# The values of cross attention: a second load from memory, or a copy on POOL

## The reference, cut to what matters

```python
q, k, v = _make_heads(_layernorm(x), H), _make_heads(ctx, H), _make_heads(ctx, H)
u = jnp.einsum('hbqd,hbkd->hbqk', q, k) * scale / np.sqrt(d_k)
logits = jnp.where(mask, -jnp.inf, jnp.tanh(u) * jnp.exp(log_C))
attn = jax.nn.softmax(logits, axis=-1)
out = jnp.einsum('hbqk,hbkd->hbqd', attn, v)        # heads joined, then @ W_out.T
x = x + out
# FFN of _layernorm(x), three times: out = out + coupling * _twist(out); then x = x + out
```

## Time and profile before

| | us |
|---|---|
| median of 3 runs (1096.41 to 1098.4) | 1096.48 |
| the profiled execution | 1098.4 |
| its span in the trace | 1096.6 |
| ACT busy | 920.6 |
| POOL busy | 554.1 |
| DMA queue of SP: packets, MB | 191008, 50.31 |
| `va` load: issues, KB each, median us from issue to landing | 64, 120.0, 3.6 |
| `cbuf` load, the same | 64, 120.0, 2.8 |

### The profile page before, as it was taken

How to read it: one execution, slowest core, us unless ns; L and a number is a source line. 1 busy time by engine, 2 the same in 40 slices (tenths; PEclk the granted TensorE clock), 3 DMA queues, 4 the chain that set the end, 5 groups by cost and what they waited for, 6 DMA issues and landing times.

```text
span 1096.6 us, 21849 instructions
## 1 busy us (share of the span) xinstructions
PE 979.9 (89%) x7260; PEld 530.3 (48%) x7260; DVE 808.9 (74%) x1738; ACT 920.6 (84%) x1153; POOL 554.1 (51%) x1053
## 2 busy tenths in 40 slices
PE   6899989899998999999999998989999899896993
PEld 4455435554355544554345543555435554453431
DVE  3888596985868666885869849698487867687285
ACT  3899778997799977998789977899779997795675
POOL 3367504884068810897028950488406881078104
PEclk7899999999999999999999999999999999998997
DMA  5433001430034200441005310143003420021002
GB/s 119 82 58 61 1 2 39 105 86 0 2 72 100 58 1 2 96 92 41 2 1 121 90 19 2 40 104 86 0 2 73 99 58 1 1 53 40 0 1 78
DMA packets 191119, 51.71 MB, mean 47 GB/s; under 512 B 165920, under 2 KB 174624, under 8 KB 191008
## 3 DMA queue, kind: packets, MB, share of 16 engines
q1 hardware_dynamic: 191008, 50.31, 21.6%
HBM read 33.37 MB, written 16.78 MB: 46 GB/s over the span
## 4 chain that ended last, share of the span: by engine, by line
ACT 41%; PE 30%; issue 13%; DVE 10%; SPq 2%; POOL 2%; DMA 1%; DVEq 0%; ACTq 0%; POOLq 0%
ACT probs L880 18%; ACT probs L886 14%; PE ps L1205 7%; PE ps L1192 6%; PE ps L1179 5%; ACT f_t L896 4%; PE ps L1116 3%; PE ps L1235 2%; DVE move_u L747 2%; DVE move_v L749 2%; PE ps L1214 2%; ACT h L912 2%; DVE f_t L753 2%; DVE coup L734 2%; PE ps L1147 1%
## 5 line engine op out<-in xcount | busy, mean ns | idle before, releaser
L880 ACT ACTIVATE probs<-ps,u_scale 120x2048 f32<-120x2048 f32 x128 | 257.6, 2012 | 21.4 <-PE ps L1116 21.4
L886 ACT ACTIVATE probs<-probs,exp_bias,clip 120x2048 f32<-120x2048 f32 x128 | 275.0, 2149 | 0.1
L1205 PE MATMUL ps<-h,w 128*128 128x512 f32 x384 | 184.4, 606 | 12.9 <-ACT h L912 12.1
L1116 PE MATMUL ps<-q_t,k_t 32*120 32x256 f32 x2048 | 150.0, 407 | 34.6 <-ACT probs L880 33.1
L475 POOL TENSOR_TENSOR c<-tok_c 128x16 f32<-128x16 f32 x8 | 1.8, 224 | 329.3 <-issue 329.3
L1147 PE MATMUL ps<-wo_t,of_t 128*128 128x256 f32 x512 | 144.5, 405 | 1.8 <-DVE xy L703 1.8
L678 DVE STREAM_TRANSPOSE o_t<-ps 128x512 f32<-128x512 f32 x128 | 90.8, 709 | 74.5 <-PE ps L1132 74.2
L1132 PE MATMUL ps<-probs,va 120*32 120x256 f32 x2048 | 138.4, 388 | 2.0 <-ACT probs L886 2.0
L1116 PEld LDWEIGHTS ps<-q_t,k_t 32*120 32x120 f32 x2048 | 95.1, 181 | 65.0 <-issue 60.5
L1147 PEld LDWEIGHTS ps<-wo_t,of_t 128*128 128x128 f32 x512 | 87.3, 190 | 51.0 <-issue 42.1
L1205 PEld LDWEIGHTS ps<-h,w 128*128 128x128 f32 x384 | 66.8, 188 | 87.7 <-issue 64.4
(11 more groups left out here) (128 smaller groups left out, 1826.5 us busy)
## 6 DMA issues: line engine op xcount, KB each, us to landing
xy<-in_x_dram SPq DMA_DIRECT2D x64, 256.0 KB, 3.3
out_dram<-xy SPq DMA_DIRECT2D x64, 256.0 KB, 2.0
cbuf<-in_ctx_dram SPq DMA_DIRECT2D x64, 120.0 KB, 2.8
va<-in_ctx_dram SPq DMA_DIRECT2D x64, 120.0 KB, 3.6
tok_c<-coup SPq DMA_DIRECT2D x256, 0.5 KB, 2.0
move_v<-in_L_xattn_W_out_dram SPq DMA_DIRECT2D x1, 256.0 KB, 5.6
move_u<-in_L_ffn_cn_w_dram SPq DMA_DIRECT2D x1, 256.0 KB, 3.4
w<-in_L_ffn_cn_w_dram SPq DMA_DIRECT2D x1, 128.0 KB, 3.1
```

The source lines that it names most:

```text
L880: eng.activation(probs[:, b % 2, n * HALF:(n + 1) * HALF, :].rearrange("k h q -> k (h q)"), banks(SCORE_BANK, 4)[0:KEYS, :], ACT.Tanh, sca ...
L886: eng.activation(p, p, ACT.Exp, scale=clip[0:KEYS, 0:1], bias=exp_bias[:, b:b + 1]).then_inc(s_exp, 1)
L1116: last = eng.matmul(banks(SCORE_BANK + r)[0:KEYS, odd * S:(odd + 1) * S], k_t[rows, b % 2, odd, n, :], q_t[rows, b % 2, n, :], start=True, ...
L1205: last = eng.matmul(banks(bank), w2[:, k, :], h1[:, p % 2, k, :], start=(k == 0), stop=(k == EK - 1))
```

## The change

`load_values` is gone from SP. POOL gets a step `values(b)`, one `tensor_scalar` that multiplies the batch's context in `cbuf` by 1.0 and writes it into `va`. In slot `i` it makes `values(i + 1)`, behind the late parts and in front of `q_hat`. It waits until the context has landed and until the products of batch `b - 3` have been made, since `va` has three buffers now in place of four. `s_va` is one semaphore that POOL counts up. SP's context load of batch `b` waits for the copy of batch `b - 4` besides the key transposes, since the copy reads `cbuf`.

```diff
-    VR = 4
-        va = sb("va", [KEYS, VR, H, SLOT])
+        va = sb("va", [KEYS, 3, H, SLOT])
-        s_va = [sem(f"s_va{n}") for n in range(VR)]
+        s_va = sem("s_va")
...
                 if b >= NLOAD:
                     eng.wait_ge(s_ktr, b - NLOAD + 1)
+                    eng.wait_ge(s_va, b - NLOAD + 1)
                 eng.dma_start(cbuf[:, b % NLOAD, :], ctx[b]).then_inc(s_ldc[b % NLOAD], 16)
-            def load_values(b):
-                if b < VR:
-                    eng.wait_ge(s_pool0, 7)
-                else:
-                    eng.wait_ge(s_pv, 2 * (b - VR + 1))
-                eng.dma_start(va[:, b % VR, :, 0:DH], ctx[b].rearrange("k (h d) -> k h d", d=DH)) \
-                   .then_inc(s_va[b % VR], 16)
...
                     load(2)
-                    load_values(0)
                     for dst, src in weight_loads:
...
                 late = late[1:]
-                if 0 < i + 2 < NB:
-                    load_values(i + 2)
...
+            def values(b):
+                eng.wait_ge(s_ldc[b % NLOAD], 16 * (b // NLOAD + 1))
+                if b >= 3:
+                    eng.wait_ge(s_pv, 2 * (b - 2))
+                eng.tensor_scalar(va[:, b % 3, :, 0:DH], cbuf[:, b % NLOAD, :].rearrange("k (h d) -> k h d", d=DH),
+                                  1.0, None, ALU.mult).then_inc(s_va, 1)
...
                 late = late[2:] if after_ffn(i) else late[1:]
+                if 0 <= i + 1 < NB:
+                    values(i + 1)
                 if new is not None and 2 <= new < NB:
                     query_hat(new)
...
                 eng.wait_ge(s_exp, 2 * b + n + 1)
-                eng.wait_ge(s_va[b % VR], 16 * (b // VR + 1))
+                eng.wait_ge(s_va, b + 1)
```

More of the change, by code:

```diff
@@ L1132, in weighted_values @@
                         last = eng.matmul(banks(PV_BANKS[n])[j * SLOT:(j + 1) * SLOT, (c % 2) * S:(c % 2 + 1) * S],
-                                          va[:, b % VR, h, :], probs[:, b % 2, h, :], start=True, stop=True,
+                                          va[:, b % 3, h, :], probs[:, b % 2, h, :], start=True, stop=True,
                                           tile_position=(0, j * SLOT))
```

## The result

| | before | after |
|---|---|---|
| median, us | 1097.23 (1096.41 to 1098.4, 4 runs) | 1111.67 (1111.09 to 1113.73, 4 runs) |
| ratio, 95% interval | | 1.0134 [1.0116, 1.0152] |
| profiled execution; its span, us | 1098.4; 1096.6 | 1110.33; 1108.5 |
| mean copy, ns (0.55 us forecast) | | 877 |

The forecast was 1097.6 with a range to 1102.6. The changed kernel is 14.4 us slower and outside it. (Differences in us between kernels are those of their medians throughout.

A forecast was written before the change was run, and what follows sets the result against it. ACT was taken to set the pace in attention, with POOL 7.5 us free per stretch. The start's -2.9 and the late slots' +4.0 gave +1.1 us, a median of 1097.6 us, range 1093.4 to 1102.6.

The forecast's parts named there:

- Part 3: POOL gains 64 copies at 0.55 us, mostly in idle time; late `q_hat` costs 0.66 us in six groups, 4.0 us.
- The upper bound of 1.11 us: Highest price considered for one POOL copy, from the slowest `q_hat` step, 1106 ns; left out of the forecast range.
- The first rival: Late slots: POOL and DVE exclude each other or short runs cost more; copy 0.9 us, +5.3 us, 1101.8; chance 0.27.
- The formula: Second late slot: ACT late by two copy prices less 0.44 us, so 0.66 us a group, 4.0 us over six.
- v: Price of one POOL copy: 0.55 us taken, 0.45 to 0.7 in the forecast's own range.
- The start: Without SP's first values transfer, later weight loads start 3.4 us earlier and batch 1's scores and tanh gain 2.9 us.
- the third rival: The start gives only SP's own time, 1.07 us; +2.9 us in sum, 1099.4; chance 0.09.
- Part 2: SP's context load also waits for the copy of four batches before; priced at nothing.
- The place: Two late slots per group: PE waits for `q_hat`, and ACT has two short waits of about 0.3 us each.
- the second rival: Late slots absorb copies of only 0.25 us, or POOL's wait moves; -2.9 us, 1093.6; chance 0.19.
- Part 4: DVE's multiply and POOL hold each other up in late slots; nothing added, up to 0.5 us per copy in the range.

The follow-up runs named there:

- e12: Kernel before with eight forms of a 120x256 POOL instruction, four times each, ahead of all other work; only durations are read; 1110.89 us.
- e6: Changed kernel with the copy as multiply by 1.0 and add 0.0, two constants instead of one; 1095.84 us, ratio to before 0.9988.
- e2: Kernel before, SP still loading values, plus a flat POOL copy with per-partition scalars into an unread buffer at the change's place; 1102.93 us, ratio 1.0043.
- e13: e9 plus six identity transposes on PE in the wait for `q_hat` in the two late slots; 1103.69 us, ratio to before 1.0064.
- e11: Changed kernel plus six identity transposes on PE ahead of the wait for `q_hat` in slots 6 and 7; 1105.36 us, ratio to before 1.0076.
- e9: Kernel before plus the 0.86 us copy into an unread buffer, only in slots 5 and 6 behind an FFN; 1110.99 us, ratio 1.0135.
- e4: Kernel before without any load of values and without a copy, output not the reference's; 1093.36 us, ratio 0.9964.
- e5: Kernel before with only the load of batch 0's values moved behind the weight loads; 1093.8 us, ratio 0.9969.
- e1: Kernel before plus seven forms of the copy on POOL behind each FFN's last low half, into an unread buffer; 1095.99 us, one run.

## Why the prediction was wrong

**The step that failed is the price of the copy in Part 3.** "The nearest is the `q_hat` step [...] I take 0.55." It measured 0.86. The nearest row was a `tensor_scalar` of the same size, but with two scalars from SBUF; the change's has one constant and no second operand, which costs twice as much as with two constants (e12, e6). The upper bound of 1.11 us contained it, but as the exception of a `q_hat`, not as the price of a form. The first rival had the price right (0.9) and the cause wrong: it blamed DVE and short runs.

**The formula was right where it applies.** Two copies late, less 0.44 of slack, six times: 4.0 forecast, 5.1 measured with a 0.55 copy (e2, interval 2.6 to 6.8), and 1.0 a group against 1.28 with the dear one in the late slots alone (e13). With v = 0.86 it gives 7.7 - 2.9 = +4.8 us, 1101.3 from the prediction's 1096.48, inside the range. So the price alone does not explain the miss. Two things that the prediction put at nothing made it 14.4:
- *The clock.* The prediction costed PE's wait by its length. At up to 1.0 us in before and up to 1.6 in e2 no fall follows it; at 1.8 us the work behind it sometimes runs at 1.2 GHz, for 0.5 to 1.9 us of ACT's time. Filling the wait took away 6.3 us (after against e11) and 7.3 (e9 against e13); that all of it is the clock is shown for the profiled executions only.
- *The backlog.* "In the other slots the copy falls in front of a wait for statistics" is the step that failed here. POOL's waits behind the copies of slots 2, 3 and 4 are the 0.59, 0.85 and 0.83 us shown above, 2.27 in all, and those three copies are 2.6. So nothing is left over at 0.55 us a copy, and 0.3 at 0.86: POOL's `f_hat` of slot 5 starts 3.37 us ahead of ACT's tanh in before (351.61, 354.98) and 3.08 in after (350.77, 353.85). Of the 7.5 us free in the earlier trace rows, 6.0 were in brackets, but 3.8 lay ahead of 331, and slots 6 and 7 had none. On the way the copies make `f_hat` late in slot 4 (PE's 0.20 at 343.66), and in slot 6 PE waits 1.76 us, 1.10 more than in the earlier trace rows: one copy of 0.86 and what was left over. In the shown group ACT's three gaps in brackets come to 1.19 us, its tanh from 345.45 to 367.63 need 22.18 us where they needed 20.61 (346.59 to 367.20), 1.57 more. The stretch ahead of them takes 0.4 more and that behind them 0.1 less, and together that is the 1.87 by which this step grew (131.85 against 129.98). Without the middle copies the same step grew by 1.04 (e13).

The ledger, in the profiled executions: start -3.9, six groups with POOL late 11.4 (e11's steps), 3.8 more for after's own (all but 0.5 of it in the three with a fall), last step 0.9: +12.1 as in the table above. The medians lie 14.4 apart; where the 2.3 us between come from is open.

**Right:**
- The start. 2.9 us forecast; 2.8 at the tanh, 3.9 at the first gelu (2.7 between the medians of seven executions each), 4.5 and 3.4 in whole runs (e4, e5). The strided transfer did hold the load behind it (0.39 us instead of 2.80), so that the third rival (1.07 us) is out.
- Part 2. No wait for `va` appears on PE, and SP's 173.9 us of waiting cost nobody anything.
- The place: the two late slots, with `q_hat` on PE and short waits of ACT. PE's wait grew to 18.3 us, near the forecast's 16, but that is luck: in a group without a fall it grew by 1.10 and 1.09 us in the two slots, against 0.55 and 0.60 forecast, and in the two groups with a fall in slot 6 the second wait is all but gone (none at 232.81, 0.18 us at 629.96).
- That nothing is gained in the steady state by a lighter DMA load: e4's steps are before's.

**Absorption**, the second rival, is what e6 nearly shows: at 0.40 us a copy the steps grow by at most 0.29, where the formula says 0.36. **The contention** of Part 4 costs nothing new: the pair that took 1.53 us beside DVE in before was the x part (362.27), in after it is `twisted` in its stead, 1.53 to 1.63 us (361.17 in the same slot).

**Left open:** why one constant costs twice as much as two; by what the chip decides when the clock falls, since the same wait of 1.86 us is followed by a fall in one group and not in another; where the last 2.3 us of the medians come from; and why the step of the fifth group is 0.6 longer in before and in most of the kernels here.

## What to carry to other kernels

Before work is moved to another engine, its price is measured in the very form in which it will be issued: an operand more or less changed this copy from 0.86 to 0.41 us, and the verdict with it. Idle time has to be read in the slots where the work lands, not in the total, and a wait that grows on TensorE may be followed by a half-speed stretch that costs as much as the wait (0.5 to 1.9 us here). And a cheap gain may sit in the order alone: one transfer in many small pieces, moved behind the weights, gave 3.4 us, about the whole profit of the change.

## What the runs showed of the hardware

- POOL's price for 120x256 elements goes by the instruction's form and not by the layout: 0.85 us (multiply by one constant), 0.41 (two constants), 0.56 (two scalars from SBUF), 0.40 (copy), flat or in runs of 16 (e12).
- Beside DVE's products of two SBUF tiles (e1), the strided copy took 0.73 instead of 0.40, the two-constant form 0.72 instead of 0.41 and the strided scalar form 1.38 instead of 0.56; the first two forms, which ran while DVE was idle, were unchanged at 0.85 and 0.87. The Trainium skill, "SBUF — State Buffer", section "Who interferes with whom", says that such DVE instructions contend with POOL's reads; e1 agrees, though overlap was not varied by itself. In the changed kernel it was no part of the loss: its copies were in the median 0.01 us above the quiet ones.
- The clock fell also without a copy. In the profiled execution of e5 PE had two waits of 1.32 and 0.57 us in an FFN, and then four products took 3.63 us where they take 1.95 in before; the step of that group was 132.32 and not 130.33:

```profile
159.27 0.70 PE L1232 MATMUL ps<-h,w4rep 64*128 64x256 f32 x4 [1.32 <-ACT h L954]
160.55 3.63 PE L1205 MATMUL ps<-h,w 128*128 128x512 f32 x4 [0.57 <-ACT h L912]
```

- Six transposes of the identity, 0.88 us, in a wait of 1.86 us were enough that no fall was seen in any group of the profiled executions of e11 and e13.
